# A token-routed expert kernel: tile coefficients picked on ScalarE by expert numbers held in registers, and one empty item left out

## The chip, the cores and the metric

The kernel runs on one core of one Trainium2 chip. The metric is the device time of one execution in microseconds (us). Engines go by the names of the profile: PE is TensorE (matmul) and PEld its weight load, DVE is VectorE, ACT is ScalarE, POOL is GpSimd, SP is SyncE, which here only issues transfers.

## What is computed

For each of 16 x 1024 tokens of width 512: a layernorm; a fixed spectral filter, after which 24 thresholded bits are error-corrected and expanded back to 512 values; and a mixture of 8 experts (512 x 512 each), of which a token uses its best two. The output is `x + s * silu(ffn)`.

```python
logits = x @ router_w.T
probs = jax.nn.softmax(logits, axis=-1)
topk_vals, topk_idx = jax.lax.top_k(probs, K_TOP)          # K_TOP = 2 of 8 experts
topk_w = topk_vals / (topk_vals.sum(-1, keepdims=True) + 1e-06)
...
xn = _layernorm(x, axis=-1)
s = _L0_attn_ref(xn, ...)       # filter, 24 bits, Golay correction, x1 + corrected @ W_le + b_le
g = _silu(_L0_ffn_ref(xn, L0_ffn_router_w, L0_ffn_expert_weights))
x = x + s * g
```

## The kernel before

The work has three stages.

**Routing** (to about 275 us). All tokens are read once; each token's two experts, its weights per expert and its bits are written to a table in HBM (`token_info`), and the tokens are sorted by their unordered pair of experts, of which there are 28. Sorted, they fill 128 tiles of 128 tokens. A main tile is computed with two experts only; where a tile holds tokens of more than one pair, the rest comes from extra items.

**Extra items** (about 275 to 396 us). There are 28 items, one for each pair in `PATH`, each with one expert. An item n gathers 128 token rows (`xbuf`, line 529) and their table rows (`inf`, line 531) on POOL into slot n % 4; DVE folds the rows into sums and differences (`halves_of`, lines 1221 to 1225); ACT rounds them to f16 (`high_part`, line 716) and DVE makes the remainder (`low_part`, line 1231); PE transposes both (`turn_extra`, line 1446), ACT copies the result out of PSUM (`turned_copy`, line 721), PE multiplies by the expert's weights in 12 matmuls (lines 1435 to 1437), ACT scales the product by a per-token coefficient in `cab` (line 737), and DVE adds it to a running sum (line 1251), which SP stores in HBM. The coefficient of an item is one column of the item's table row times one column of `tq`; POOL computes it (`extra_coef`, line 545), one item ahead, just before it gathers. A gather into a slot waits for the coefficient and the remainder of the slot's old item (`coef_ready`, `split_ready`). In the same stage DVE still makes the low halves of the weights (`low_parts`, two instructions of 128x1024, lines 908 and 915), in the order `EXPERT_ORDER`, some of them before the first item and some at the items that `LOW_AT` names.

**Main tiles** (about 396 to 1228 us). A loop over 128 tiles, four to a round. PE reads the tile's two expert numbers from `tile_exp` into registers (`value_load`, line 1460), multiplies by both experts (24 matmuls) and by the filter and bit tables (13 more). DVE combines the two products with the tile's two coefficients `cab[:, k, 0:2]` (lines 1265 and 1274). Those coefficients are made two tiles ahead in two steps: POOL multiplies a mark table `onehot` (128 tiles x 2 experts x 8, with the unscaling of the expert in place of the one) by the 8 weights in the table row (`main_coef`, line 553), and DVE sums over the 8 (line 1239). The mark table itself is built by DVE in the stage of the extra items, in two instructions of 128x2048 elements (`marks_alike`, line 1202, after item 14, and `marks_scaled`, line 1209, after item 18). In each main step POOL adds the input to the result (line 569), multiplies marks (line 553), gathers the rows of four tiles later (lines 529 and 531) and scatters the output (line 535). ACT runs, per step, `high_part`, a copy out of PSUM (line 746), the silu (line 750), the bits (line 707), and the two one-column copies of indices `sidx` (line 755) and `gidx` (line 710), for which POOL's scatter and gather wait.

The engines run their programs in order and meet through semaphores; nothing reorders them. SP transposes the f16 parts of main tiles (`DMA_TRANSPOSE`) and loads the extra sums.

Of the kernel before, what the change touches and what calls it, by code (L numbers as in the profile page):

```python
# [8 lines left out]
F16 = mybir.dt.float16  # L9
# [7 lines left out]
P = 128  # L17
# [61 lines left out]
def build(nc, x_in, W_el, b_el, W_le, b_le, router_w, experts, consts, out):  # L79
# [39 lines left out]
    with ctx:  # L119
# [3 lines left out]
        def sem(name):  # L123
# [61 lines left out]
        tdiag = sb("tdiag", [P, 2, P], F16)  # L185
# [4 lines left out]
        ctmp = sb("ctmp", [P, 2, 2, NE])  # L190
# [58 lines left out]
        onehot = xT4[:, :, :, :].rearrange("p b c n -> p (b c n)")[:, 0:T * 2 * NE].rearrange(  # L249
            "p (t s e) -> p t s e", s=2, e=NE)  # L250
# [11 lines left out]
        z2, t2, g2 = (two(arena, 2 * E * i) for i in range(3))  # L262
        NB = 2 * C + 1
        HB = NB * P // 2
        part_at = (17 * E, 17 * E + HB, 6 * E, 7 * E)
        turn_at = (17 * E + 2 * HB, 17 * E + 3 * HB, 8 * E, 9 * E)
        parts = [arena[:, a:a + (HB if r < 2 else E)].bitcast(F16) for r, a in enumerate(part_at)]
        facing = [arena[:, a:a + (HB if r < 2 else E)].bitcast(F16).rearrange("p (m n) -> p m n", n=P) for r, a in enumerate(turn_at)]
# [19 lines left out]
        def sems(names):  # L288
# [3 lines left out]
        pool_halves, live_ready, marks_ready = sems("pool_halves live_ready marks_ready")  # L292
# [25 lines left out]
        rows_ready, rows_loaded, rows_float, exps_mm, toks_mm, diag_ready, spread_mm, tiles_ready = sems(  # L318
            "rows_ready rows_loaded rows_float exps_mm toks_mm diag_ready spread_mm tiles_ready")
# [7 lines left out]
        coef_mul, coef_sum, coef_ready, x_done, x_scaled, acc_init, acc_ready = sems("coef_mul coef_sum coef_ready x_done x_scaled acc_init acc_ready")  # L327
# [42 lines left out]
        def extra(i):  # L370
            return isinstance(i, int) and i < XR

# [98 lines left out]
        def _(pool):  # L471
# [67 lines left out]
            def extra_coef(n):  # L539

                k = n % U
                pool.wait_ge(ld_x2[k], 32 * (n // U + 1))
                after(pool, x_scaled, n - U + 1)
                c = 8 + PATH[n][1]
                G.tensor_tensor(cab[:, k, 0:1], inf2[:, k, c:c + 1], tq[:, 7, n:n + 1], ALU.mult).then_inc(coef_ready, 1)

            def main_coef(i, k):

                m = (i - XR) * U + k
                pool.wait_ge(ld_x2[k], 32 * (i + 1))  # L550
                if not (first_main(i) and k < 2):
                    pool.wait_ge(coef_sum, m - 1)
                G.tensor_tensor(ctmp[:, k % 2], onehot[:, bass.ds(m, 1)].rearrange("p o s e -> p (o s) e"),
                                inf2[:, k, 8:8 + NE].unsqueeze(1).broadcast_to([P, 2, NE]), ALU.mult).then_inc(coef_mul, 1)

            def extra_prepare(n):
                if n + 1 < NX:
                    extra_coef(n + 1)
                pool.wait_ge(gidx_ready, n + U + 1)
                pool.wait_ge(split_ready, n + 1)  # L560
                pool.wait_ge(coef_ready, n + 1)
                gather(n % U)

            def step(i, k, last=False):
# [5 lines left out]
                if not (last and k + 2 >= U):  # L570
                    main_coef(*at(i, k, 2))
# [8 lines left out]
            for k in range(U):  # L580
                pool.wait_ge(gidx_ready, k + 1)
                gather(k)
            pool.wait_ge(live_ready, 1)
            extra_coef(0)
            for n in range(NX):
                extra_prepare(n)
            pool.wait_ge(marks_ready, 2)
            main_coef(XR, 0)
            main_coef(XR, 1)
# [5 lines left out]
        def _(act):  # L595
# [107 lines left out]
            def bits_part(i, k):  # L703
                b = k % 2
                act.wait_ge(ld_x2[k], 32 * (i + 1))
# [11 lines left out]

            def turned_copy(n):
# [5 lines left out]
            def extra_step(n):  # L724
                k, b = n % U, n % 2
                if 0 < n < NX - 1:
                    turned_copy(n + 1)
# [11 lines left out]
            def step(i, k, last=False):  # L739
# [19 lines left out]
            for k in range(U):  # L759
                gather_index(0, k)  # L760
            act.wait_ge(pad_ready, 1)
            for k in range(3):
                high_part(0, k)
                gather_index(1, k)
                if k == 1:
                    turned_copy(0)
                    turned_copy(1)
            for n in range(NX):
                extra_step(n)
            main_rounds(act, step)  # L770

        @block.vector
        def _(dve):
# [399 lines left out]
            V.memset(again[:, 0:1], 0.0)  # L1173
            V.tensor_scalar(tdiag[:, 0], ident[:, :], tsel[:, 0, 2:3], None, ALU.mult)
            V.tensor_scalar(tdiag[:, 1], ident[:, :], tsel[:, 0, 3:4], None, ALU.mult)
            link(V.tensor_tensor(count, to_tile[:, 0, 0:NX], iota_c[:, 0:NX], ALU.mult))
            V.tensor_reduce(tslot[:, :], count, AXX, ALU.max).then_inc(diag_ready, 1)
# [15 lines left out]
            for c in range(2):  # L1193
                low_parts(c)
            V.memset(acc2[:, 1], 0.0).then_inc(acc_init, 1)

            def marks_alike():
# [3 lines left out]
                dve.wait_ge(spread_mm, 1)  # L1201
# [318 lines left out]
```

## Time and profile before

| | |
|---|---|
| median of 3 runs | 1231.86 us (1228.46 to 1235.25) |
| the profiled execution | 1235.18 us, its span 1233.3 us |
| busy, share of the span | PE 92%, DVE 89%, POOL 71%, ACT 42%, PEld 49% |
| mean granted clock of PE | 0.969 |

Times in the rows below are from the start of the span of the profiled execution. The shares are means over stages that have different limits, so the stages are read one by one.

### The profile page before, as it was taken

To read this page: it belongs to the slowest core of one execution; us is meant where nothing else is said; L and a number is where in the kernel's file an instruction comes from. 1 tells how busy PE (TensorE), PEld (TensorE's weight loads), DVE (VectorE), ACT (ScalarE), POOL (GpSimd) and SP (SyncE) were. 2 spreads that over 40 slices of the span, in tenths; PEclk is the share of its full clock that TensorE was granted. 3 is DMA by queue.
4 is the path that set the end of the run, shared out by engine and by line. 5 is a ranking of instruction groups with operands and counts; after the bars stand their busy time and mean duration, and the time that the engine had idled before them with its cause. 6 is when DMAs were issued, how large, how long until landed. Compare 5 with 4: busy or idle time off the path is not lost. (4 is left out here: it accounts for less than half of the span.)

```text
span 1233.3 us, 26827 instructions
## 1 busy us (share of the span) xinstructions
PE 1131.4 (92%) x6283; PEld 609.0 (49%) x6284; DVE 1096.8 (89%) x2658; ACT 512.7 (42%) x1151; POOL 877.7 (71%) x857
## 2 busy tenths in 40 slices
PE   5998869725889999999999999999999999999996
PEld 4565545412434455555555555555555555555553
DVE  6899969998877889899989998999999899999985
ACT  4476646664655333333333333333333333333332
POOL 1136655648886588777878887888888788888874
PEclk9999989957999999999999999999999999999999
DMA  8669999403446576666667666666666666666663
GB/s 322 242 212 200 198 149 203 81 23 97 150 144 175 147 172 171 171 174 173 174 166 179 173 173 166 176 174 176 172 169 176 171 175 173 170 178 172 174 167 108
DMA packets 216921, 208.74 MB, mean 169 GB/s; under 512 B 166271, under 2 KB 166271, under 8 KB 212786
## 3 DMA queue, kind: packets, MB, share of 16 engines
q1 hardware_dynamic: 184370, 124.31, 42.8%
q0 software_dynamic: 31360, 79.78, 21.9%
q10 hardware_dynamic: 1152, 4.19, 1.3%
q8 instruction: 17, 0.28, 0.1%
q14 instruction: 22, 0.18, 0.1%
HBM read 123.36 MB, written 47.11 MB: 138 GB/s over the span
## 5 line engine op out<-in xcount | busy, mean ns | idle before, releaser
L1435 PE MATMUL banks<-w_hi,arena 128*128 (+1 forms) x1136 | 432.5, 381 | 6.2 <-DMA arena<-arena 5.9
L1436 PE MATMUL banks<-w_lo,arena 128*128 (+1 forms) x1136 | 432.3, 381 | 0.0
L1437 PE MATMUL banks<-w_hi,arena 128*128 (+1 forms) x1136 | 432.2, 380 | 0.0
L716 ACT ACTIVATE arena<-xbuf,inf 128x512 f16<-128x512 f32 x156 | 112.6, 722 | 532.5 <-DVE xbuf L1225 532.2
L529 POOL DMA_INDIRECT xbuf<-in_L_attn_x,gidx x156 | 189.7, 1216 | 78.9 <-issue 66.2
L531 POOL DMA_INDIRECT inf<-token_info,gidx x156 | 200.2, 1283 | 54.0 <-issue 53.4
L508 POOL DMA_INDIRECT pair_tokens<-tok,slot x112 | 112.6, 1005 | 110.4 <-DVE slot L1058 78.4
L569 POOL TENSOR_TENSOR xbuf<-xbuf 128x512 f32<-128x512 f32 x128 | 162.8, 1272 | 35.8 <-DVE xbuf L1294 28.7
L1435 PEld LDWEIGHTS banks<-w_hi,arena 128*128 128x128 f16 x1136 | 111.4, 98 | 134.3 <-issue 17.1
L1437 PEld LDWEIGHTS banks<-w_hi,arena 128*128 128x128 f16 x1136 | 111.5, 98 | 131.5 <-issue 1.7
L535 POOL DMA_INDIRECT out<-xbuf,sidx x128 | 142.6, 1114 | 40.7 <-issue 40.4
L1436 PEld LDWEIGHTS banks<-w_lo,arena 128*128 128x128 f16 x1136 | 111.3, 98 | 117.7 <-issue 1.7
L1221 DVE TENSOR_TENSOR xbuf<-xbuf 128x256 f32<-128x256 f32 x156 | 141.1, 905 | 25.3 <-DMA inf<-token_info,gidx 25.1
L1231 DVE SCALAR_TENSOR_TENSOR arena<-xbuf,inf,arena 128x512 f16<-128x512 f32 x156 | 117.1, 750 | 17.2 <-ACT arena L716 11.5
L1369 PE MATMUL banks<-xT,wcat 128*128 128x512 f32 x256 | 119.8, 612 | 0.8 <-issue 0.4
L1274 DVE SCALAR_TENSOR_TENSOR arena<-banks,cab,arena 128x512 f32<-128x512 f32 x128 | 95.6, 747 | 14.2 <-PE banks L1437 12.2
L1294 DVE TENSOR_TENSOR xbuf<-xbuf,arena 128x512 f32<-128x512 f32 x128 | 88.7, 693 | 17.0
L1265 DVE SCALAR_TENSOR_TENSOR arena<-banks,cab,arena 128x512 f32<-128x512 f32 x128 | 95.9, 749 | 7.3 <-DMA arena<-extra_sums 4.0
L1288 DVE TENSOR_TENSOR xbuf<-xbuf 128x256 f32<-128x256 f32 x256 | 97.5, 422 | 4.4
L928 DVE BATCH_NORM_STATS2 st<-xbuf 128x6 f32<-128x512 f32 x128 | 85.8, 682 | 11.4 <-DMA xbuf<-in_L_attn_x 11.4
L1329 PE MATMUL banks<-ident,xbuf 128*128 128x128 f32 x512 | 73.8, 292 | 22.0 <-DMA xbuf<-in_L_attn_x 21.7
L750 ACT ACTIVATE arena<-arena,inf 128x512 f32<-128x512 f32 x128 | 91.2, 712 | 3.3 <-DVE arena L1274 3.3
(305 smaller groups left out, 1728.7 us busy)
## 6 DMA issues: line engine op xcount, KB each, us to landing
xbuf<-in_L_attn_x SPq DMA_DIRECT2D x32, 1024.0 KB, 11.1
arena<-extra_sums SPq DMA_DIRECT2D x128, 256.0 KB
arena<-in_L_ffn_expert_weights SPq DMA_DIRECT2D x8, 1024.0 KB, 11.0
extra_sums<-arena SPq DMA_DIRECT2D x28, 256.0 KB, 2.9
token_info<-info ACTq DMA_DIRECT2D x8, 512.0 KB, 11.5
xbuf<-in_L_attn_x,gidx POOLq DMA_INDIRECT x156
inf<-token_info,gidx POOLq DMA_INDIRECT x156
arena<-arena SPq DMA_TRANSPOSE x128
```

What stands on the lines that cost most here:

```text
L508: pool.indirect_dma_start(out=pair_slots, out_offset=bass.IndirectOffsetOnAxis(ap=slot[:, buf, t:t + 1], axis=0), in_=tok[:, buf, t:t + 1] ...
L529: pool.indirect_dma_start(out=x2[:, k], out_offset=None, in_=x_rows, in_offset=tokens, bounds_check=N - 1, oob_is_err=False).then_inc(ld_x ...
L531: pool.indirect_dma_start(out=inf2[:, k], out_offset=None, in_=info_dram, in_offset=tokens, bounds_check=N - 1, oob_is_err=False).then_inc ...
L535: pool.indirect_dma_start(out=out_rows, out_offset=bass.IndirectOffsetOnAxis(ap=sidx[:, k:k + 1], axis=0), in_=o2[:, k % 2], in_offset=Non ...
L569: G.tensor_tensor(o2[:, b], sg2[:, b], x2[:, k], ALU.add).then_inc(o_ready, 1)
L716: nc.scalar.activation(hi4[ring(i, k)], uv2[:, b], ACT.Copy, scale=inf2[:, k, 1:2]).then_inc(hi_ready, 1)
L1221: V.tensor_tensor(raw2[:, b, 0:H], x2[:, k, 0:H], x2[:, k, H:E], ALU.add).then_inc(raw_ready, 1)
L1231: V.scalar_tensor_tensor(lo4[ring(i, k)], uv2[:, b], inf2[:, k, 1:2], hi4[ring(i, k)], ALU.mult, ALU.subtract).then_inc(split_ready, 1)
L1369: last = mm(psum[:, 2], wcat[:, c], xT4[:, k % 2, c], start=(c == 0), stop=(c == C - 1))
L1435: mm(ps, hi[:, c], wh, start=(c == 0), stop=False)
L1436: mm(ps, hi[:, c], wl, start=False, stop=False)
L1437: end = mm(ps, lo[:, c], wh, start=False, stop=(c == C - 1))
```

## The change

1. The coefficients of extra items and of main tiles move from POOL to ACT. For an extra item it is one copy of a column with a per-token scale. For a main tile ACT loads each of the two expert numbers into a register and copies column `8 + e` of the table row, scaled by `unscale[:, e]`. There is no sum on DVE for it any more.
2. The mark table is gone: the two DVE instructions that build it, the two that prepare it, one matmul, and 128 multiplications on POOL and 128 sums on DVE.
3. Item 0 (the pair of experts 0 and 1, for which no tokens are ever left over) isn't computed. Its semaphores are counted up, its sum is a memset, and `EXPERT_ORDER` and `LOW_AT` start with expert 2. POOL's first gather is item 1's, and the gather of item 4 goes into the unused slot 0.
4. Some buffers move into the place of the mark table (`xT4`).

```diff
-    EXPERT_ORDER = (*range(1, NE), 0)
-    DIFF_AT = (6, 1, 3, 4, 5, 0, 2, 7)
-    LOW_AT = {1: 4, 2: 5, 3: 6, 9: 7}
+    EXPERT_ORDER = (*range(2, NE), 1, 0)
+    DIFF_AT = (6, 7, 1, 3, 4, 5, 0, 2)
+    LOW_AT = {1: 4, 2: 5, 3: 6, 12: 7}
...
-            def extra_prepare(n):
-                if n + 1 < NX:
-                    extra_coef(n + 1)
+            def extra_gather(n):
+
                 pool.wait_ge(gidx_ready, n + U + 1)
                 pool.wait_ge(split_ready, n + 1)
                 pool.wait_ge(coef_ready, n + 1)
...
                 G.tensor_tensor(o2[:, b], sg2[:, b], x2[:, k], ALU.add).then_inc(o_ready, 1)
-                if not (last and k + 2 >= U):
-                    main_coef(*at(i, k, 2))
                 pool.wait_ge(sidx_ready, m + 1)
...
+            def extra_coef(n):
+
+                k, c = n % U, 8 + PATH[n][1]
+                act.wait_ge(ld_x2[k], landed(n // U, k))
+                after(act, x_scaled, n - U + 1)
+                nc.scalar.activation(cab[:, k, 0:1], inf2[:, k, c:c + 1], ACT.Copy, scale=tq[:, 7, n:n + 1]).then_inc(coef_ready, 1)
+
+            def main_coef(i, k):
+
+                m = (i - XR) * U + k
+                act.wait_ge(ld_x2[k], landed(i, k))
+                if first_main(i):
+                    act.wait_ge(x_scaled, NX - U + k + 1)
+                else:
+                    act.wait_ge(z_ready, m - U + 1)
+                for c in range(2):
+                    e = act.value_load(tile_exp[0:1, c, bass.ds(m, 1)], min_val=0, max_val=NE - 1)
+                    nc.scalar.activation(cab[:, k, c:c + 1], inf2[:, k, bass.ds(e + 8, 1)], ACT.Copy,
+                                         scale=unscale[:, bass.ds(e, 1)]).then_inc(coef_picked, 1)
...
                 elif n + 3 < NX + 2:
                     bits_part(*at(n // U, k, 3))
+                if n + 1 < NX:
+                    extra_coef(n + 1)
                 act.wait_ge(x_done, n + 1)
...
                     bits_part(*at(i, k, 2))
+                    main_coef(*at(i, k, 2))
...
-            def marks_scaled():
-
-                dve.wait_ge(marks_ready, 1)
-                V.tensor_tensor(onehot, onehot, unscale[:, :].unsqueeze(1).unsqueeze(1).broadcast_to([P, T, 2, NE]),
-                                ALU.mult).then_inc(marks_ready, 1)
...
-            for k in range(3):
-                halves_of(0, k)
-                low_part(0, k)
-                if k:
-                    low_parts(k + 1)
-            halves_of(0, 3)
-            for n in range(NX):
+            halves_of(0, 1)
+            halves_of(0, 2)
+            low_part(0, 1)
+            low_part(0, 2)
+            low_parts(1)
+            halves_of(0, 3)
+            low_parts(2)
+            low_part(0, 3)
+            low_parts(3)
+            halves_of(1, 0)
+            for n in range(1, NX):
                 extra_step(n)
```

**POOL in the stage of the extra items.** Before, three rows per item, with the coefficient of the next item first:

```order
50 L545 TENSOR_TENSOR cab<-inf,tq 128x1 [waits ld_x2_2]
51 L529 DMA xbuf<-in_L_attn_x,gidx 128x512 [waits coef_ready,split_ready,gidx_ready]
52 L531 DMA inf<-token_info,gidx 128x64
53 L545 TENSOR_TENSOR cab<-inf,tq 128x1 [waits ld_x2_3]
54 L529 DMA xbuf<-in_L_attn_x,gidx 128x512 [waits coef_ready,split_ready,gidx_ready]
55 L531 DMA inf<-token_info,gidx 128x64
```

Now, where the first three gathers wait only for indices:

```order
42 L531 DMA xbuf<-in_L_attn_x,gidx 128x512 [waits gidx_ready]
43 L533 DMA inf<-token_info,gidx 128x64
44 L531 DMA xbuf<-in_L_attn_x,gidx 128x512 [waits coef_ready,split_ready,gidx_ready]
45 L533 DMA inf<-token_info,gidx 128x64
46 L531 DMA xbuf<-in_L_attn_x,gidx 128x512 [waits coef_ready,split_ready,gidx_ready]
47 L533 DMA inf<-token_info,gidx 128x64
```

The multiplication is gone from POOL, and `coef_ready`, which POOL itself used to fulfil, is now fulfilled by ACT.

**ACT in the same stage.** One item before (its place in the steady part, from the copy of the transposed parts on):

```order
250 L721 ACTIVATE arena<-banks 128x1024 [waits x_done,uvT_done]
251 L716 ACTIVATE arena<-xbuf,inf 128x512 [waits uvT_done,uv_ready]
252 L710 ACTIVATE gidx<-tile_tok 128x1
253 L737 ACTIVATE arena<-banks,cab 128x512 [waits acc_ready,coef_ready,x_done]
254 L721 ACTIVATE arena<-banks 128x1024 [waits x_done,uvT_done]
```

The same now:

```order
252 L718 ACTIVATE arena<-banks 128x1024 [waits x_done,uvT_done]
253 L693 ACTIVATE xT<-xbuf,inf 128x512 [waits uvT_done,uv_ready]
254 L687 ACTIVATE gidx<-tile_tok 128x1
255 L700 ACTIVATE cab<-inf,tq 128x1 [waits x_scaled,ld_x2_1]
256 L736 ACTIVATE xT<-banks,cab 128x512 [waits acc_ready,coef_ready,x_done]
```

The coefficient of item n + 1 now stands behind the rounding (`high_part`) of item n + 3, and ahead of the scaling of item n.

**ACT in the loop over main tiles.** One step before:

```order
404 L716 ACTIVATE arena<-xbuf,inf 128x512 [waits turned1,uv_ready]
405 L743 REGISTER_ALU
406 L746 ACTIVATE xbuf<-banks 128x384 [waits s_ready,y_done]
407 L750 ACTIVATE arena<-arena,inf 128x512 [waits sg_ready,z_ready]
408 L707 ACTIVATE arena<-inf 128x96 [waits turned1,ld_x2_1]
409 L755 ISA [waits stored1]
410 L755 ACTIVATE sidx<-tile_tok 128x1
411 L710 ISA
412 L710 ACTIVATE gidx<-tile_tok 128x1
```

Now, from the bits on:

```order
469 L684 ACTIVATE arena<-inf 128x96 [waits turned1,ld_x2_3]
470 L711 ISA [waits z_ready,ld_x2_3]
471 L711 TENSOR_LOAD tile_exp
472 L711 ISA x2
473 L712 ISA
474 L712 ACTIVATE cab<-inf,unscale 128x1
475 L711 ISA
476 L711 TENSOR_LOAD tile_exp
477 L711 ISA x2
478 L712 ISA
479 L712 ACTIVATE cab<-inf,unscale 128x1
480 L755 ISA [waits stored1]
```

Two loads into a register, some register instructions and two one-column copies stand between the bits and the copies of the indices.

## Rows read from the trace of the kernel before

**Rows 1.** Busy time by stretch: length, then busy and count per engine, clock, DMA

```profile
396.00:1222.00 826.00, 821.21 (x4723) 429.56 (x4723) 751.74 (x1649) 275.11 (x758) 646.76 (x627) 1.00 0.67 171
275.50:393.20 117.70, 93.89 (x562) 45.54 (x561) 98.14 (x210) 67.55 (x115) 101.80 (x93) 0.91 0.46 135
```

**Rows 2.** Groups of ACT, 440 to 1200 us: busy, mean ns, idle before

```profile
L716 ACT ACTIVATE arena<-xbuf,inf 128x512 f16<-128x512 f32 x118 | 85.2, 722 | 457.8 <-DVE xbuf L1225 457.8
```

**Rows 3.** One main step, timeline: start, length, engine

```profile
703.77 0.19 ACT L710 ACTIVATE gidx<-tile_tok 128x1 int32 x1
707.73 0.72 ACT L716 ACTIVATE arena<-xbuf,inf 128x512 f16<-128x512 f32 x1 [3.76 <-DVE xbuf L1225]
...
706.54 0.40 POOL L553 TENSOR_TENSOR ctmp<-xT,inf 128x16 f32<-128x16 f32 x1
707.47 1.15 POOL L529 DMA_INDIRECT xbuf<-in_L_attn_x,gidx  x1 [0.52 <-issue]
```

**Rows 4.** Loads of a register from `tile_exp`, min/median/max ns (lines 1460, 451)

```profile
L1460 PEldq TENSOR_LOAD <-tile_exp x256: 294/344/1192, 390.8 to 1215.4; - x128
L451 SPq FUSED_REGOPS  x248: 46/155/187, 400.9 to 1215.1; - x124
L451 SPq TENSOR_LOAD <-tile_exp x128: 283/728/1049, 400.4 to 1214.6; - x128
```

**Rows 5.** Groups in 315 to 349 us: busy, mean ns, idle before

```profile
L531 POOL DMA_INDIRECT inf<-token_info,gidx x11 | 13.9, 1263 | 3.4 <-issue 3.4
L529 POOL DMA_INDIRECT xbuf<-in_L_attn_x,gidx x10 | 13.7, 1368 | 1.5
...
L545 POOL TENSOR_TENSOR cab<-inf,tq 128x1 f32<-128x1 f32 x10 | 4.0, 395 | 0.3
```

**Rows 6.** Timeline of one extra item, POOL, DVE and ACT

```profile
337.15 1.37 POOL L529 DMA_INDIRECT xbuf<-in_L_attn_x,gidx  x1
338.82 1.02 POOL L531 DMA_INDIRECT inf<-token_info,gidx  x1 [0.30 <-issue]
...
341.65 0.43 DVE L1221 TENSOR_TENSOR xbuf<-xbuf 128x256 f32<-128x256 f32 x1 [0.89 <-DMA inf<-token_info,gidx]
...
342.92 0.72 ACT L716 ACTIVATE arena<-xbuf,inf 128x512 f16<-128x512 f32 x1 [1.06 <-DVE xbuf L1225]
343.55 0.19 ACT L710 ACTIVATE gidx<-tile_tok 128x1 int32<-128x1 int32 x1
343.64 0.67 ACT L737 ACTIVATE arena<-banks,cab 128x512 f32<-128x512 f32 x1
```

**Rows 7.** Timeline of DVE: the first folding instruction of five items

```profile
314.31 0.42 DVE L1221 TENSOR_TENSOR xbuf<-xbuf 128x256 f32<-128x256 f32 x1
...
348.28 0.42 DVE L1221 TENSOR_TENSOR xbuf<-xbuf 128x256 f32<-128x256 f32 x1 [0.97 <-DMA inf<-token_info,gidx]
...
373.05 0.43 DVE L1221 TENSOR_TENSOR xbuf<-xbuf 128x256 f32<-128x256 f32 x1 [0.69 <-DMA inf<-token_info,gidx]
...
389.07 0.42 DVE L1221 TENSOR_TENSOR xbuf<-xbuf 128x256 f32<-128x256 f32 x1 [0.34 <-DMA inf<-token_info,gidx]
```

**Rows 8.** Timeline around the two mark instructions, DVE and POOL

```profile
351.21 2.27 DVE L1202 TENSOR_TENSOR xT<-banks,cst 128x2048 f32<-128x2048 f32 x1
...
353.57 5.73 POOL L529 DMA_INDIRECT xbuf<-in_L_attn_x,gidx  x1
...
367.61 2.29 DVE L1209 TENSOR_TENSOR xT<-xT,unscale 128x2048 f32<-128x2048 f32 x1
...
368.24 3.21 POOL L531 DMA_INDIRECT inf<-token_info,gidx  x1 [0.31 <-issue]
```

**Rows 9.** Timeline of the first items: POOL, then DVE

```profile
276.90 1.95 POOL L531 DMA_INDIRECT inf<-token_info,gidx  x1 [0.30 <-issue]
281.55 1.00 POOL L531 DMA_INDIRECT inf<-token_info,gidx  x1 [0.31 <-issue]
284.25 1.50 POOL L531 DMA_INDIRECT inf<-token_info,gidx  x1 [0.30 <-issue]
...
302.22 1.28 DVE L908 SCALAR_TENSOR_TENSOR w_lo<-w_lo,wscale,w_hi 128x1024 f16<-128x1024 f32 x1
303.42 1.27 DVE L915 SCALAR_TENSOR_TENSOR w_lo<-arena,wscale,w_hi 128x1024 f16<-128x1024 f32 x1
```

**Rows 10.** Timeline, ACT's last scaling and DVE's first work on a main tile

```profile
394.51 0.69 ACT L737 ACTIVATE arena<-banks,cab 128x512 f32<-128x512 f32 x1 [1.90 <-PE banks L1437]
403.98 0.75 DVE L1265 SCALAR_TENSOR_TENSOR arena<-banks,cab,arena 128x512 f32<-128x512 f32 x1 [3.96 <-DMA arena<-extra_sums]
```

More of the change, by code:

```diff
@@ L261, in build @@
         yp2 = raw2[:, :, H:E]
-        z2, t2, g2 = (two(arena, 2 * E * i) for i in range(3))
+        z2, g2 = (two(arena, 2 * E * i) for i in range(2))
+        t2 = two(spare, 4 * E)
         NB = 2 * C + 1
         HB = NB * P // 2
[L265 to L268, printed above, removed]
+        part_at = (17 * E, 17 * E + HB, 0, E)
+        turn_at = (17 * E + 2 * HB, 17 * E + 3 * HB, 2 * E, 3 * E)
+        parts = [(arena[:, a:a + HB] if r < 2 else spare[:, a:a + E]).bitcast(F16) for r, a in enumerate(part_at)]
+        facing = [(arena[:, a:a + HB] if r < 2 else spare[:, a:a + E]).bitcast(F16).rearrange("p (m n) -> p m n", n=P)
+                  for r, a in enumerate(turn_at)]
         hi4, lo4 = [t[:, 0:E] for t in parts], [t[:, E:2 * E] for t in parts]
@@ L371, in extra, with landed @@
             return isinstance(i, int) and i < XR
+        def landed(i, k):
+            return 32 * (i + (1 if k else 0))
         def ring(i, k):
@@ L579, in step @@
                 scatter_out(k)
-            for k in range(U):
+            for k in range(1, U):
                 pool.wait_ge(gidx_ready, k + 1)
                 gather(k)
-            pool.wait_ge(live_ready, 1)
-            extra_coef(0)
             for n in range(NX):
[L586 to L589, printed above, removed]
+                extra_gather(n)
             main_rounds(pool, step)
@@ L758, in _ @@
             act.wait_ge(tiles_ready, 1)
-            for k in range(U):
+            act.sem_inc(gidx_ready, 1)
+            for k in range(1, U):
                 gather_index(0, k)
+            gather_index(1, 0)
+            act.sem_inc(coef_ready, 1)
+            act.sem_inc(hi_ready, 1)
+            act.sem_inc(hl_ready, 1)
+            act.sem_inc(x_scaled, 1)
             act.wait_ge(pad_ready, 1)
-            for k in range(3):
+            act.wait_ge(live_ready, 1)
+            for k in range(1, U):
                 high_part(0, k)
                 gather_index(1, k)
-                if k == 1:
-                    turned_copy(0)
+                if k == 2:
                     turned_copy(1)
-            for n in range(NX):
+                    turned_copy(2)
+            extra_coef(1)
+            for n in range(1, NX):
                 extra_step(n)
+            act.wait_ge(tiles_ready, 2)
+            main_coef(XR, 0)
+            main_coef(XR, 1)
             main_rounds(act, step)
@@ L1277, in step @@
                     low_part(*at(i, k, 2))
-                if not (last and k + 1 >= U):
-                    main_coef(*at(i, k, 1))
                 dve.wait_ge(y_copied, m + 1)
@@ L1486, in step @@
                 end.then_inc(y_done, 1)
-            turn_extra(0)
-            for n in range(NX):
+            pe.sem_inc(uvT_done, 1)
+            pe.sem_inc(x_done, 1)
+            turn_extra(1)
+            for n in range(1, NX):
                 extra_step(n)
```

76 lines of the change are left out of this document (20 added, 56 removed).

## The prediction

> **What bounds the kernel now.** I read the busy time by stretch first, because the page's shares mix three stages. In the main tiles (396 to 1222 us) PE is busy 821.21 of 826 us at full clock, DVE 751.74, POOL 646.76 and ACT 275.11 [rows 1]. The reader is to see that 4.8 us is all that any change off PE can win there, over 128 tiles of 6.45 us. In the extra items (275.5 to 393.2 us) no engine stands at its limit by busy time: PE 93.89 of 117.7, DVE 98.14, POOL 101.80, ACT 67.55. So I went to the groups and the timeline. In the quiet part POOL's only idle time is what the profile calls issue, some 0.3 us before line 531 and nothing to speak of before line 529, while DVE waits for the rows to land, 0.89 us ahead of the item shown [rows 5, 6]. POOL is the bound there, through the time it takes to issue two gathers and one small multiplication. The first folding instruction of an item recurs from 314.31 to 348.28 us ten times over: 3.40 us an item [rows 7]. That is also POOL's sum, 1.37 + 1.26 + 0.40 us of work and some 0.4 us of idle, 3.4 us.
>
> Two places are slower. Up to 314 us DVE is the bound, since it also makes low halves of weights, 2.4 us per expert. Around the mark table the six items from 348.28 to 373.05 us take 24.8 us, 4.13 each [rows 7]: a gather that takes 1.0 us undisturbed lasts 5.73 us right behind the first mark instruction, and another 3.21 us beside the second [rows 8].
>
> **The change, part by part.**
>
> *Main tiles: what leaves.* POOL loses line 553, 0.40 us a step, and DVE its sum of 0.16 us. PE is the bound, so both are worth nothing except where PE waits now, inside the 4.8 us. I take 1 us (bounds 0 and 3).
>
> *Main tiles: what comes.* ACT gets two picks per step. No row shows a pick on ACT. Its parts are a register load, at 0.34 us in the median on PE's sequencer and 0.73 us on SP's, register instructions of 0.05 to 0.16 us, of which there are about three to a pick [rows 4], and a one-column copy, 0.19 us in the index copies [rows 3]. So a pick is between 0.34 + 0.15 + 0.19 = 0.7 us and 1.05 + 0.5 + 0.19 = 1.7 us; I take 1.1, since SP's load feeds the same sort of address arithmetic, and two picks make 2.2 us. Behind them on ACT are the two index copies, for which POOL waits, and then the next step's rounding, for which DVE, SP's transposition and PE wait. The index for the gather is ready at 703.96 us now and would be at 706.2; POOL starts that gather at 707.47 and without line 553 at about 707.0 [rows 3]. The rounding finds ACT idle for 3.76 us in that step, and 457.8 us over 118 steps, 3.88 on average [rows 2, 3]. So two picks are hidden, by 0.8 us on POOL's side and 1.6 on PE's. A gather that comes late by a few tenths feeds a tile four steps later, so the second margin is the one that counts. Cost 0.
>
> *Marks.* DVE loses 2.27 + 2.29 us and two small preparations, and the stretched gathers have nothing to follow. Against the quiet 3.40 us, six items save 24.8 - 20.4 = 4.4 us. The lower bound is 0, if the stretched gathers come from DVE's other work in a row.
>
> Here the Trainium skill is to be weighed. Its page "SBUF — State Buffer", section "SBUF: two separate sides", says that DVE and GpSimd take a shared pair of ports by an exclusive lock for one instruction at a time, and that descriptor writing is kept out by DVE's two-port modes. The row shows 4.7 us of extra time in one gather, twice as long as any one DVE instruction near it, and the first mark instruction had ended before, so a lock held by that one instruction doesn't explain it. If the lock of whatever follows does, the marks matter only by crowding DVE, and the 4.4 us could stay partly in the program: that is the first case of the rival "nothing" below.
>
> *Coefficients of extra items.* POOL loses 28 multiplications of 0.40 us with some 0.15 us around each. If POOL stayed the bound, an item would take 3.40 - 0.5 = 2.9 us. But the gather of item n + 4 waits for the coefficient of item n, which on ACT now stands behind the rounding of item n + 2, and that needs the rows of item n + 2 landed. This is a loop over two items. Its parts: from the end of POOL's line 531 at 339.84 us to DVE's first folding at 341.65, 1.8 us; to ACT's rounding at 342.92, 1.27 us; rounding 0.63 us and index copy 0.09 us until the next instruction starts [rows 6]; the coefficient 0.19 us and a semaphore 0.1 us. That is 4.1 us from the end of one gather to the start of the one two later. The two gathers themselves take 1.37 + 0.30 + 1.02 = 2.7 us there [rows 6], 2.35 undisturbed (1.02 for line 529, as it is in its shortest form). An item takes half the loop: (4.1 + 2.7) / 2 = 3.40 us, between 3.2 and 3.6. So the new wait gives back what the multiplication costs: the releaser of POOL changes, and the pace doesn't. From item 8 to the end of the stage, 21 items, that is 0 (bounds -4 and +4 us); the last five items ran at 16.0 / 5 = 3.2 us before [rows 7], which would be 1 us lost.
>
> *Item 0 and the start.* POOL's first three gathers keep their places; their second halves end at 278.85, 282.55 and 285.75 us [rows 9] and land 1.8 us later, now as items 1 to 3. DVE, in the new order: folding of item 1 from 280.7; of item 2 from 284.4 to 285.6 (it waits for the landing, 2.5 us that item 0's work filled before); two remainders to 287.1; an expert's low halves, 2.4, to 289.5; folding of item 3, 1.2, to 290.7; low halves to 293.1; remainder to 293.8; low halves to 296.2; folding of item 4 to 297.3; folding of item 5, whose gather starts after ACT's coefficient at 291.8 and lands at 296, to 298.5; remainder and sum to 299.8. That point is at 302.22 us now, where line 908 starts [rows 9]. Gain 2.4 us (bounds 1 and 4), less than an item's 3.4, because the start waits for transfers.
>
> *The end of the stage.* ACT's four picks for the first two main tiles start behind its last scaling, which ends at 395.2, and take 4.4 us, and the first sum on DVE that uses them starts at 403.98, held by a transfer [rows 10]. Hidden; without that wait they would cost up to 1 us.
>
> **Sum.** 1 + 0 + 4.4 + 0 - 1 + 2.4 = 6.8 us, taken as 7. The profiled execution took 1235.18 us around a span of 1233.3, so it becomes 1228.2; that execution lies 3.3 us above the median of the runs, 1231.86. Against the median, which I use: **1225 us**. A measurement of this kernel can tell about 0.5%, some 6 us, from no change, so the forecast lies at that edge.
>
> **The rivals.**
>
> *POOL keeps the bound and sheds it.* If landing and rounding overlap better than in the loop above, the pace falls to PE's own 3.05 us (twelve matmuls at 0.216 us and the transpositions at about 0.45), not to 2.9. 21 items x 0.35 us = 7 us more than forecast: about 1218 us. For it: POOL shows no wait but issue. Against: the loop's four durations are all in the rows.
>
> *Nothing is won.* The loop takes 3.6 us an item (+4 us) and the stretched gathers appear elsewhere (+3 us): 1231 to 1232 us. For it: other gathers of 2.7 us stand beside DVE's low halves, which stay. By the page's rule on the lock, taken by itself, the marks' time would partly stay, as said.
>
> *Slower: the picks on ACT.* If a pick takes more than 1.9 us (half of 3.8), ACT's rounding comes late, then DVE's remainder, SP's transposition and PE in every step. At 2.2 us a pick a step grows by 0.6 us: 126 x 0.6 = 76 us, less the 7 won, about 1300 us; at 2.0 us it is 1243. It decides from 1.9 us on, beyond my upper bound of 1.7. For it: no row shows a load on ACT, and one on PE took 1.19 us.
>
> *The change doesn't do what it says*: the order shows that it does, so this has no chance of its own.
>
> **How the numbers follow.** Forecast 0.52, its own range 1221 to 1229; full shedding 0.18; nothing 0.20; slower by the picks 0.10. The range of 8 in 10 goes from 1214 to 1233: it leaves out the slow case and a little below. Faster than 1225.7 holds six tenths of the forecast and the shedding case, 0.49; within 0.5% the rest of the forecast and the case of nothing less a tail, 0.39; slower 0.12.
>
> **What the profile of the changed kernel would show.** Right: the stage of extra items 6 to 7 us shorter, POOL now waiting before line 529 for ACT, an item still near 3.4 us, no gather beyond 3.5 us after 349 us; in the main tiles the same 6.4 us a step, ACT waiting some 1.6 us before its rounding. Wrong: POOL without waits and items near 3.05 us; or ACT not idle before the rounding and PE with gaps in each main step; or gathers of 3 to 6 us still there.

## The result, and the profile after it

The changed kernel is slower. Its median is 1239.88 us (1235.3 to 1243.27) beside 1231.92 us (1227.79 to 1237.16) for the kernel before, a ratio of 1.0066 with a 95% interval of 1.0041 to 1.0091, so 8 us lost where 7 were forecast to be won.

The stage of the extra items is read first, with two rows of the timeline that bound it, POOL's first gather and PE's first matmul of a main tile:

```profile
271.98 1.01 POOL L531 DMA_INDIRECT xbuf<-in_L_attn_x,gidx  x1 [7.95 <-ACT gidx L687]
399.04 0.39 PE L1422 MATMUL banks<-w_hi,arena 128*128 x1 [2.94 <-DMA arena<-arena]
```

The stage takes 127.06 us; before, the same two instructions stood at 275.58 and 395.89, 120.31 us. So 6.75 of the 8 us of loss are here. "The stage" means this length from here on. (The routing ahead of it differs by 3.6 us between the two profiled executions, the other way.) The groups of POOL and DVE in 315 to 385 us:

```profile
L533 POOL DMA_INDIRECT inf<-token_info,gidx x18 | 22.0, 1224 | 5.5 <-issue 5.5
L531 POOL DMA_INDIRECT xbuf<-in_L_attn_x,gidx x18 | 17.9, 997 | 25.1 <-ACT cab L700 22.3 <-issue 2.7
...
L1218 DVE TENSOR_TENSOR xbuf<-xbuf 128x256 f32<-128x256 f32 x18 | 7.6, 422 | 23.7 <-DMA inf<-token_info,gidx 23.7
```

Against [rows 5] POOL has lost the line of multiplications and got 22.3 us of waiting for ACT's coefficient (line 700) in 18 items, and DVE waits as long for the rows to land. No engine is at its limit now; the stretch by engine (length, then busy and count of PE, PEld, DVE, ACT and POOL, clock, DMA):

```profile
318.00:389.00 71.00, 56.59 (x363) 28.61 (x362) 47.20 (x112) 45.98 (x91) 40.34 (x37) 1.00 0.47 144
```

The timeline of two items shows the wait and what it hangs on. POOL's rows, then DVE's and ACT's of the item between:

```profile
349.39 0.99 POOL L531 DMA_INDIRECT xbuf<-in_L_attn_x,gidx  x1 [2.50 <-ACT cab L700]
350.68 1.44 POOL L533 DMA_INDIRECT inf<-token_info,gidx  x1 [0.30 <-issue]
352.43 1.00 POOL L531 DMA_INDIRECT xbuf<-in_L_attn_x,gidx  x1 [0.30 <-issue]
353.73 1.00 POOL L533 DMA_INDIRECT inf<-token_info,gidx  x1 [0.30 <-issue]
357.25 1.00 POOL L531 DMA_INDIRECT xbuf<-in_L_attn_x,gidx  x1 [2.52 <-ACT cab L700]
```

```profile
354.11 0.43 DVE L1218 TENSOR_TENSOR xbuf<-xbuf 128x256 f32<-128x256 f32 x1 [2.40 <-DMA inf<-token_info,gidx]
...
355.37 0.72 ACT L693 ACTIVATE xT<-xbuf,inf 128x512 f16<-128x512 f32 x1 [2.33 <-DVE xbuf L1222]
...
356.00 0.18 ACT L687 ACTIVATE gidx<-tile_tok 128x1 int32<-128x1 int32 x1
...
356.09 0.28 ACT L700 ACTIVATE cab<-inf,tq 128x1 f32<-128x1 f32 x1
```

Every second gather of rows waits: 349.39, 357.25, and on with 7.7 to 8.0 us between them, 7.86 here, which is 3.93 us an item instead of the 3.40 of [rows 7]. The loop closes as the prediction described it: the gather ends at 352.12, lands and is folded from 354.11, rounded from 355.37, its index copied, the old item's coefficient made from 356.09 to 356.37, and the next gather starts at 357.25.

The main tiles are unchanged. PE is busy all the time between 420 and 1215 us, and ACT's two picks stand in the step with room behind them:

```profile
420.00:1215.00 795.00, 793.18 (x4571) 415.61 (x4570) 720.96 (x1482) 327.70 (x983) 595.14 (x494) 1.00 0.68 173
```

```profile
701.89 0.28 ACT L712 ACTIVATE cab<-inf,unscale 128x1 f32 x1
702.44 0.29 ACT L712 ACTIVATE cab<-inf,unscale 128x1 f32 x1 [0.27 <-issue]
702.64 0.19 ACT L755 ACTIVATE sidx<-tile_tok 128x1 int32 x1
702.74 0.19 ACT L687 ACTIVATE gidx<-tile_tok 128x1 int32 x1
705.95 0.72 ACT L693 ACTIVATE arena<-xbuf,inf 128x512 f16<-128x512 f32 x1 [3.03 <-DVE xbuf L1222]
```

Two picks put off the index by 0.85 us (701.89 to 702.74) and leave 3.03 us of waiting before the rounding, where [rows 3] had 3.76.

### The profile page after: what moved, and what is told of

Its sections match the earlier page's. It is cut to its first block and busy times, and to the rows that moved or that the text cites. A ratio compares the mean times of both kernels' runs of the same rounds, so it can differ in the third digit from the quotient of the medians.

```text
span 1238.1 us, 27677 instructions
## 1 busy us (share of the span) xinstructions
PE 1128.5 (91%) x6262; PEld 606.6 (49%) x6263; DVE 1077.8 (87%) x2519; ACT 577.9 (47%) x1431; POOL 808.5 (65%) x699
## 5 line engine op out<-in xcount | busy, mean ns | idle before, releaser
L1422 PE MATMUL banks<-w_hi,arena 128*128 (+1 forms) x1076 | 410.1, 381 | 8.1 <-DMA arena<-arena 7.1
L1423 PE MATMUL banks<-w_lo,arena 128*128 (+1 forms) x1076 | 409.5, 381 | 0.0
L1424 PE MATMUL banks<-w_hi,arena 128*128 (+1 forms) x1076 | 409.4, 381 | 0.0
L693 ACT ACTIVATE arena<-xbuf,inf 128x512 f16<-128x512 f32 x141 | 101.8, 722 | 407.7 <-DVE xbuf L1222 407.6
L531 POOL DMA_INDIRECT xbuf<-in_L_attn_x,gidx x155 | 173.9, 1122 | 161.1 <-POOL xbuf L553 96.8
L1422 PEld LDWEIGHTS banks<-w_hi,arena 128*128 128x128 f16 x1076 | 105.6, 98 | 130.9 <-issue 18.6
L1424 PEld LDWEIGHTS banks<-w_hi,arena 128*128 128x128 f16 x1076 | 105.7, 98 | 124.4 <-issue 1.9
L1423 PEld LDWEIGHTS banks<-w_lo,arena 128*128 128x128 f16 x1076 | 105.5, 98 | 112.2 <-issue 1.8
L1261 DVE SCALAR_TENSOR_TENSOR arena<-banks,cab,xT 128x512 f32<-128x512 f32 x128 | 95.9, 749 | 21.7 <-PE banks L1424 17.3
L1228 DVE SCALAR_TENSOR_TENSOR arena<-xbuf,inf,arena 128x512 f16<-128x512 f32 x141 | 105.6, 749 | 7.3 <-ACT arena L693 4.3
L1252 DVE SCALAR_TENSOR_TENSOR xT<-banks,cab,arena 128x512 f32<-128x512 f32 x128 | 95.8, 749 | 8.6 <-DMA arena<-extra_sums 6.0
L712 ACT ACTIVATE cab<-inf,unscale 128x1 f32 x256 | 73.9, 289 | 43.7 <-issue 43.3
```

What stands on the lines that cost most here:

```text
L531: pool.indirect_dma_start(out=x2[:, k], out_offset=None, in_=x_rows, in_offset=tokens, bounds_check=N - 1, oob_is_err=False).then_inc(ld_x ...
L693: nc.scalar.activation(hi4[ring(i, k)], uv2[:, b], ACT.Copy, scale=inf2[:, k, 1:2]).then_inc(hi_ready, 1)
L1228: V.scalar_tensor_tensor(lo4[ring(i, k)], uv2[:, b], inf2[:, k, 1:2], hi4[ring(i, k)], ALU.mult, ALU.subtract).then_inc(split_ready, 1)
L1422: mm(ps, hi[:, c], wh, start=(c == 0), stop=False)
L1423: mm(ps, hi[:, c], wl, start=False, stop=False)
L1424: end = mm(ps, lo[:, c], wh, start=False, stop=(c == C - 1))
```

## The experiments

Twelve kernels were run in three groups of four; the kernel before ran beside each group, and the ratio is to it. Its median was 1300.81 us in the first group, on a chip where the routing takes about 60 us longer, 1223.89 in the second and 1224.14 in the third, so times are compared within a group and ratios across them.

### The coefficient first in ACT's step (e1)

```diff
                 k, b = n % U, n % 2
+                if n + 1 < NX:
+                    extra_coef(n + 1)
                 if 1 < n < NX - 1:
                     turned_copy(n + 1)
                 if n + 3 < NX + 2:
                     high_part(*at(n // U, k, 3))
...
-                if n + 1 < NX:
-                    extra_coef(n + 1)
                 act.wait_ge(x_done, n + 1)
```

> The changed kernel with one move on ScalarE: in each step of the extra items the coefficient of item n + 1 is made first, before the copy of the transposed parts and before the rounding of item n + 3. Theory, the loop: in the changed kernel a gather waits for a coefficient that stands behind a rounding two items on, and the loop of two items takes 7.86 us. With the coefficient first the loop spans three items, so GpSimd should no longer wait some 2.5 us for it in every second item, an item should take 3.1 to 3.3 us and the stage from the first gather to PE's first main matmul should fall from 127.1 us to about 112: about 1225 us, ratio to before 0.99 to 1.00. Rival, the picks in the main tiles cost the time: nothing changes, 1240 us. Rival, something else holds the extra items (VectorE, the start without item 0): an item stays above 3.7 us.

Measured: 0.992 (0.9898 to 0.9942), stage 109.73 us. Groups of POOL in its steady stretch, 383 to 442 us:

```profile
L531 POOL DMA_INDIRECT xbuf<-in_L_attn_x,gidx x18 | 22.9, 1270 | 9.2 <-issue 6.8 <-ACT cab L700 2.1 <-DVE arena L1228 0.3
L533 POOL DMA_INDIRECT inf<-token_info,gidx x18 | 20.3, 1128 | 5.5 <-issue 5.2 <-ACT cab L700 0.3
```

The wait for ACT falls from 22.3 to 2.4 us over 18 items. The coefficient itself takes the same time (0.28 us in both kernels); only its place has changed.

### The coefficient three items ahead (e2), and back on POOL (e3)

In e2 the same call stands where the changed kernel has it, but makes the coefficient of item `n + 3`, whose own rounding it follows:

```diff
-                if n + 1 < NX:
-                    extra_coef(n + 1)
+                if n + 3 < NX:
+                    extra_coef(n + 3)
...
                 gather_index(1, k)
+                extra_coef(k)
...
-            extra_coef(1)
             for n in range(1, NX):
```

The last lines are the start of the stage, where each of the items 1 to 3 gets its coefficient behind its own rounding.

> The changed kernel, but the coefficient of item n + 3 is made right behind the rounding of the same item, two steps earlier than in the changed kernel, and at the start each of items 1 to 3 has its coefficient right behind its rounding. Loop theory: the wait is gone as in the run with the coefficient first, and at the start the gather of item 5 no longer waits 3.4 us; as fast as that run or 1 to 3 us faster, about 1223 us. Rival, picks in the main tiles: 1240 us. If this is as slow as the changed kernel and the run with the coefficient first is too, the loop theory falls.

In e3 the coefficient is POOL's again, as before, while item 0, the marks and the main picks stay changed:

```diff
             def extra_gather(n):
+                if n + 1 < NX:
+                    pool_coef(n + 1)
                 pool.wait_ge(gidx_ready, n + U + 1)
...
-                if n + 1 < NX:
-                    extra_coef(n + 1)
                 act.wait_ge(x_done, n + 1)
```

> The changed kernel with the coefficients of the extra items back on GpSimd as before the change; the picks of the main tiles stay on ScalarE, there is no mark table and no item 0. Loop theory: the multiplication of 0.4 us comes back and the wait goes, an item takes 3.4 us in the quiet part as before; with marks gone (4.4 us) and the shorter start (2 to 4 us) the stage takes about 113 us, the time is about 1225 us. Rival, the picks on ScalarE in the main tiles: 1238 us or more, with main tiles slower than 6.45 us each.

Measured: e2 0.9929 (0.9912 to 0.9947), stage 108.66 us; e3 0.9947 (0.9928 to 0.9967), stage 111.57 us. Both are rid of the loss. e3 against before also gives the terms for the marks, item 0 and the main tiles together: 5.3 parts in a thousand, 6.5 us of 1231 (4 to 9); the forecast had 4.4 + 2.4 + 1 = 7.8.

### The kernel before with the added wait alone (e4)

```diff
                 pool.wait_ge(coef_ready, n + 1)
+                pool.wait_ge(hi_ready, n + 3)
                 gather(n % U)
```

> The kernel before the change with one more wait and nothing else: GpSimd's gather of item n + 4 waits until ScalarE has rounded item n + 2. Coefficients, marks and item 0 stay as they were. Loop theory: landing 2.0 + to the rounding 1.26 + rounding 0.7 + from ScalarE's end to the start of a gather that waited 0.9 + two gathers 2.74 make 7.6 us, an item takes about 3.8 us in place of 3.40, so the kernel becomes 6 to 10 us slower than before, ratio about 1.006. Rival, the wait is harmless and the loss came with another part of the change: ratio 1.000.

Measured: 1.0066 (1.0045 to 1.0087), stage 125.65 us. Two gathers that waited, and the rounding that released the second:

```profile
378.27 1.03 POOL L529 DMA_INDIRECT xbuf<-in_L_attn_x,gidx  x1 [0.94 <-ACT gidx L711]
...
381.46 1.03 POOL L529 DMA_INDIRECT xbuf<-in_L_attn_x,gidx  x1 [0.27 <-issue]
...
383.57 0.72 ACT L717 ACTIVATE arena<-xbuf,inf 128x512 f16<-128x512 f32 x1 [1.35 <-DVE xbuf L1226]
...
385.17 1.03 POOL L529 DMA_INDIRECT xbuf<-in_L_attn_x,gidx  x1 [0.93 <-ACT gidx L711]
```

One line that computes nothing makes the kernel before as slow as the changed one. The profile puts the wait down to the index copy, which is the last thing ACT finished; what the added line waits for is the rounding, and that ends at 384.29, 0.88 us before the gather starts.

The pace isn't the one that I expected. Two items take 6.90 us here (378.27 to 385.17) and 7.03 us the next time, 3.5 us an item and not 3.8. The gather of a table row takes 1.09 us and is folded 1.62 us after its end, where my sum had 1.44 and 2.0; no run shows why they are shorter here. Of the 5.3 us by which the stage is longer, 2.2 arise at the start (the low halves of item 1 end 31.3 us after the first gather instead of 29.1), and the rest comes after the last low halves, where the kernel before had been faster than 3.40 (the last six intervals between gathers are 3.49 us on average instead of 3.13). So e4 shows that such a wait is enough for a loss of this size. It doesn't confirm the 3.93 us of the changed kernel, which rests on that kernel's own rows.

### The wait moved to the gather that needs it (e5), and the changed kernel beside it (e8)

The coefficient reads the table row, so only the gather of table rows must wait for it:

```diff
                 pool.wait_ge(split_ready, n + 1)
...
+                pool.indirect_dma_start(out=x2[:, k], out_offset=None, in_=x_rows, in_offset=tokens,
+                                        bounds_check=N - 1, oob_is_err=False).then_inc(ld_x2[k], 16)
                 pool.wait_ge(coef_ready, n + 1)
-                gather(n % U)
+                pool.indirect_dma_start(out=inf2[:, k], out_offset=None, in_=info_dram, in_offset=tokens,
+                                        bounds_check=N - 1, oob_is_err=False).then_inc(ld_x2[k], 16)
```

> The changed kernel with one wait moved: the gather of the rows no longer waits for the coefficient, only the gather of the table row does, since only that one overwrites what the coefficient reads. Theory of the loop over two items: only the table gather is then in it, 5.13 us from landing to the released gather plus 1.0 to 1.4 for the gather itself, 6.1 to 6.6 us for two items, so 3.05 to 3.3 us an item in place of 3.93, the stage 13 to 17 us shorter than that of the changed kernel (127.1), time about 0.993 to 0.996 of before. Rival: a gather that waits for another engine costs its 0.9 us whatever the loop, because POOL starts again each time; then an item still takes 3.7 us or more and the ratio is 1.002 or above.

> The changed kernel itself, unaltered, on the chip of these runs, so that the ratios of the others can be set against it. Its earlier ratio was 1.0066 of before; both theories expect 1.004 to 1.009 here, an item of 3.93 us in the steady part and a stage of about 127 us.

Measured: e5 0.99 (0.9883 to 0.9917), 1211.93 us, stage 108.94 us; e8 1.0062 (1.0045 to 1.0078), 1230.75 us, stage 127.69 us. Moving one wait by one instruction is worth 18.8 us, in the time and in the stage, a little more than the 13 to 17 that I had expected. In e5 one wait of this kind in POOL's timeline:

```profile
340.44 1.00 POOL L547 DMA_INDIRECT xbuf<-in_L_attn_x,gidx  x1 [0.30 <-issue]
342.77 1.19 POOL L550 DMA_INDIRECT inf<-token_info,gidx  x1 [1.33 <-ACT cab L705]
```

and the stretch by engine, where PE is busy for 53.35 of 55 us and is now what bounds it:

```profile
310.00:365.00 55.00, 53.35 (x344) 26.93 (x343) 44.99 (x104) 43.55 (x87) 41.13 (x35) 1.00 0.58 174
```

A released gather still costs its 0.8 us (ACT's copy ends at 342.00), so the rival, that the cost comes with each wait whatever the loop, is false: it was paid only where it stood in the loop.

### Both edits (e9), and the marks' work put back (e6 on e1, e10 on e9)

```diff
+                if n in (NX // 2, NX // 2 + 4):
+                    V.tensor_tensor(spare[:, 6 * E:8 * E].bitcast(F16).rearrange("p (t s e) -> p t s e", s=2, e=NE),
+                                    unscale[:, :].unsqueeze(1).unsqueeze(1).broadcast_to([P, T, 2, NE]),
+                                    iota_c[:, 0:NE].unsqueeze(1).unsqueeze(1).broadcast_to([P, T, 2, NE]), ALU.mult)
```

The result of these two instructions is unused.

> The version with the coefficient first in ACT's step (ratio 0.992, stage 109.7 us), with two unused DVE instructions of 128x2048 put back after items 14 and 18, where the mark table was built. My marks term of 4.4 us says: a gather of 3 to 6 us appears behind each, and the stage grows by 4 to 5 us (113.7 to 114.7), ratio about 0.9955. Rival: the stretched gathers come from DVE's work in a row whatever it is, and POOL now has slack; then the stage grows by 0 to 2 us and the ratio stays within 0.001 of 0.992.

> The changed kernel with the two edits that each took away the loop put together: the coefficient first in ACT's step, and the wait for it only before the gather of the table row. If PE's pace of 3.05 us an item is the floor in both, together they win nothing more: ratio 0.990 to 0.993, stage 108 to 110 us, no gather waiting for ACT beyond the first items. Rival: some of the wait is left in either alone; then 2 to 4 us more come off, ratio 0.987 to 0.989.

> The version with both edits, with the two unused DVE instructions of 128x2048 put back at the places where the mark table was built; run beside that version, so that the marks' price is a difference on one chip. My term of 4.4 us: stage 4 to 5 us longer than that of the version without them, ratio 0.0035 higher. Rival, that POOL's slack takes up the stretched gathers once it doesn't bound the stage: stage 0 to 2 us longer, ratio within 0.0015.

Measured: e6 0.9951 (0.9934 to 0.9968), stage 112.24 us, beside 0.992 for e1 in another group; e9 0.9915 (0.9888 to 0.9941), 1213.95 us, stage 113.31 us; e10 0.995 (0.9931 to 0.9969), 1216.65 us, stage 115.12 us. DVE's two instructions and POOL's gathers in e10:

```profile
333.06 2.27 DVE L1306 TENSOR_TENSOR xT<-unscale,cst 128x2048 f16<-128x2048 f32 x1
333.85 4.81 POOL L550 DMA_INDIRECT inf<-token_info,gidx  x1 [0.30 <-issue]
...
348.08 4.35 POOL L550 DMA_INDIRECT inf<-token_info,gidx  x1 [0.30 <-DVE arena L1233]
348.60 2.29 DVE L1306 TENSOR_TENSOR xT<-unscale,cst 128x2048 f16<-128x2048 f32 x1
```

The long gathers of [rows 8] are back, in both kernels, so this work does bring them. But they are not its alone. In e9, without any such instruction, the profiled execution has this one beside an expert's low half:

```profile
327.14 3.35 POOL L547 DMA_INDIRECT xbuf<-in_L_attn_x,gidx  x1 [0.30 <-DVE xT L1233]
327.67 1.29 DVE L931 SCALAR_TENSOR_TENSOR w_lo<-arena,wscale,w_hi 128x1024 f16<-128x1024 f32 x1
```

and its stage is 113.31 us, while e11 and e12 below, the same program up to the main tiles, have 108.02 and 107.94. So the stage scatters by 5 us between single profiles. The marks' price is 2.7 us by the medians of e9 and e10 and 4.3 by their ratios, whose intervals overlap a little. A price of 4.4 is not refuted, and not measured closely either. By its ratio e9 also wins nothing over e1 and e5, as expected if either edit alone brings the stage to PE's pace.

### More picks in the main tiles: four (e11), six (e12), ten (e7)

```diff
+                for j in range(2):          # 4 in e12, 8 in e7
+                    e = act.value_load(tile_exp[0:1, j % 2, bass.ds(m, 1)], ...)
+                    nc.scalar.activation(unused[:, k, j:j + 1], inf2[:, k, bass.ds(e + 8, 1)], ACT.Copy,
+                                         scale=unscale[:, bass.ds(e, 1)])
                 for c in range(2):
```

e11 and e12 are built on e9, e7 on e1. These picks are unused.

> The version with the coefficient first in ACT's step, with eight unused picks ahead of the two real ones in every main step (their columns go to an unused buffer). Two picks take 0.85 us in the changed kernel, so ten take 4.3 us, 3.4 us more than the real two, and ACT waits 2.8 to 3.0 us before its rounding. Theory that ACT's slack is what that wait shows: a step grows by about 0.5 us, 126 steps by 60 us, ratio 1.04. Rival one: the work ahead gives more room than that wait shows, ratio below 1.005. Rival two: POOL's gather, which waits for the index copy behind the picks, is the sooner limit, a step grows by 1 us or more, ratio above 1.08.

> The version with both edits, with two unused picks ahead of the real ones in every main step. In the version with ten picks one took 0.68 us with its idle time, so two more take 1.4 us out of some 3.0 us for which ACT waits before its rounding. Theory that this wait is ACT's slack: no change, ratio within 0.001 of the version without them, and a wait of 1.5 to 1.7 us left. Rival, that a pick delays what is behind it beyond ACT's own time (POOL's gather by the index copy): a step grows by 0.2 us or more, ratio 0.02 higher.

> The same with four unused picks, 2.7 us out of the 3.0 us. Theory: still no change beyond 0.003, a wait of 0.2 to 0.5 us left before the rounding; the limit lies between here and the ten picks. If ACT's slack is used up earlier, because the instructions of the picks hold up the ones behind them, a step grows by 0.3 us or more, ratio 0.03 higher.

Measured: e11 0.9902 (0.9873 to 0.9932), no change; e12 1.0473 (1.0448 to 1.0499); e7 1.351 (1.3479 to 1.3541). The groups of ACT in the main tiles, of e11 over 107 steps and of e12 over 99:

```profile
L699 ACT ACTIVATE arena<-xbuf,inf 128x512 f16<-128x512 f32 x107 | 77.3, 722 | 173.4 <-DVE xbuf L1232 173.4
...
L722 ACT ACTIVATE cab<-inf,unscale 128x1 f32 x216 | 63.6, 294 | 87.4 <-issue 87.4
L718 ACT ACTIVATE unused<-inf,unscale 128x1 f32 x215 | 62.0, 288 | 36.7 <-issue 36.7
```

```profile
L718 ACT ACTIVATE unused<-inf,unscale 128x1 f32 x396 | 114.1, 292 | 100.1 <-issue 99.8
L699 ACT ACTIVATE arena<-xbuf,inf 128x512 f16<-128x512 f32 x99 | 71.3, 720 | 89.7 <-DVE xbuf L1232 84.4 <-issue 5.2
...
L722 ACT ACTIVATE cab<-inf,unscale 128x1 f32 x197 | 58.0, 295 | 131.8 <-issue 131.8
```

Busy and idle time added, a step's picks cost 0.90 us for two (e9), 2.33 for four and 4.08 for six. With four, ACT waits 1.62 us before the rounding instead of 3.04, and nothing else changes. With six a step takes 0.56 us more ((1281.9 - 1210.77) / 126), which my expectation for e12 denied: 0.9 us of ACT's wait is still left, but POOL's gather now waits for the index copy behind the picks, and PE for what comes later still. Groups of POOL, DVE and PE in e12:

```profile
L532 POOL DMA_INDIRECT xbuf<-in_L_attn_x,gidx x99 | 116.7, 1179 | 155.5 <-ACT gidx L693 107.0 <-POOL xbuf L559 39.1 <-issue 9.4
...
L1228 DVE TENSOR_TENSOR xbuf<-xbuf 128x256 f32<-128x256 f32 x99 | 85.9, 868 | 83.7 <-DMA inf<-token_info,gidx 83.7
...
L1432 PE MATMUL banks<-w_hi,arena 128*128 x792 | 303.0, 383 | 40.7 <-DMA arena<-arena 39.1 <-issue 0.5
```

So POOL's side is the nearer margin, as the rows read; no run here moved the index copies ahead of the picks to prove it.

In e7 ACT itself is the bound. Its groups over 74 steps:

```profile
L713 ACT ACTIVATE unused<-inf,unscale 128x1 f32 x592 | 168.1, 292 | 236.6 <-issue 236.4
L694 ACT ACTIVATE arena<-xbuf,inf 128x512 f16<-128x512 f32 x74 | 53.1, 718 | 52.0 <-issue 50.7 <-DVE xbuf L1227 1.3
...
L717 ACT ACTIVATE cab<-inf,unscale 128x1 f32 x146 | 43.0, 295 | 59.0 <-issue 59.0
```

Of 52.0 us of idle time before its rounding 50.7 are issue, so ACT hardly waits for anyone. A pick there costs 0.69 us, not the 0.43 from which I had expected 60 us. Ten picks take 6.9 us a step, 6.0 more than two, and the idle time before the rounding falls from 3.04 to 0.70 us. That makes 3.7 us more, about the 3.5 us by which a step is longer than in e5 ((1652.69 - 1211.93) / 126). The ratio is the one that my second rival had asked for (above 1.08), but its reason, POOL's gather as the sooner limit, is not what these rows show.

## Why the prediction was wrong, point by point

**The step that failed** is the loop in *Coefficients of extra items*. "The coefficient 0.19 us and a semaphore 0.1 us. That is 4.1 us from the end of one gather to the start of the one two later" and from it "the releaser of POOL changes, and the pace doesn't". The form of the loop was right, instruction for instruction. Its size was not: from 352.12 to 357.25 it is 5.13 us. Landing took 1.99 us for 1.8, folding 1.26 for 1.27, rounding and index copy the 0.72 foretold, the coefficient 0.28 for 0.19, and from its end to the start of the gather 0.88 us for 0.1. With the two gathers and the 0.30 us between them, 2.73 us, that is 7.86 us for two items, 3.93 us each. The 0.88 us is the largest part of what was missing, 0.8 of 1.0 us, and half of it an item. It stood in the trace of before, in two rows that I didn't quote, where a gather waits for ACT's index copy:

```profile
274.48 0.48 ACT L710 ACTIVATE gidx<-tile_tok 128x1 int32<-128x1 int32 x4 [3.30 <-DVE tile_tok L1169]
275.58 1.02 POOL L529 DMA_INDIRECT xbuf<-in_L_attn_x,gidx  x1 [8.74 <-ACT gidx L710]
```

The four copies run from 274.48 to 274.96. The first gather needs only the first of them, which ends at 274.68, and it starts 0.90 us after that, 0.62 us after the end of the last. I had taken 0.1 us from no row at all. With 0.6 to 0.9 the loop would have come out at 3.65 to 3.8 us an item, 5 to 8 us over 21 items, and the forecast at no change.

0.53 us on the 23 items from item 5 on is 12.2 us. This is an estimate: from the gather of item 13 to that of item 27 an item takes 3.93 us, but before that DVE's low halves set part of the pace in both kernels. Between the end of the low halves at item 1 and the first main matmul the forecast had 3.4 us won; it was 10.6 lost. So the loop is some 12 us of a miss of 14.0 us; the rest I didn't take apart. That the loop and nothing else turned the sign is shown by e1, e2 and e5, each of which breaks it in another way, leaves the rest of the change as it is, and lands at 0.990 to 0.993. e4 adds that such a wait alone can cost as much.

**"POOL keeps the bound and sheds it"**, 1218 us, described what happens once the loop is away: PE's own pace. e5 stands 12 us below before, where that rival had 14.

**"Nothing is won"** named the right mechanism, a loop of more than 3.40 us an item, and gave it 3.6; the place was right and the size short again.

**Marks**, 4.4 us: their stretched gathers are away in the changed kernel (none over 1.53 us after 349 us), and come back with the work. By e3 this, the start and the main tiles are worth 6.5 us together. **Item 0 and the start**, 2.4 us: the end of item 1's low halves is 25.3 us after the first gather and was 29.1, 3.8 us won, inside its bounds. **Main tiles, what leaves**, 1 us: not seen; from first to last main matmul 829.2 us beside 827.7, where single profiles scatter by as much. **What comes**, 0: right. I had put two picks at 2.2 us where they take 0.9, and e11 shows that 2.3 us would have been hidden too. **"Slower: the picks on ACT"** put its threshold at 3.8 us for a step's picks; e12 has 4.08 and is slower, so the limit was near where it was said to be, but the changed kernel is nowhere near it. As the rows of e12 read, it was reached on POOL's side, by the late index, which the prediction had said would not count. The example in that rival is also added up wrongly: at 2.0 us a pick it should be 0.2 x 126 = 25 us, less the 7, so 1250 us and not 1243.

## What to carry to other kernels

When work moves to another engine, a slot's release moves with it: draw the loop from the release through the transfer and back, and price each handover in it by a row in which that very kind of instruction waits for another engine. Then ask which of the waiting instructions really overwrites what is read; here the first of two gathers waited for a reader of the second, and one line was worth 18.8 us. In a program in order, put a short instruction on which another engine waits ahead of the long one that waits itself.

## What the hardware showed that I had not expected

- A gather on POOL that has waited for ACT in the extra items starts 0.88 us after the end of the instruction that releases it in the changed kernel (all 13 times) and in e4, 0.76 to 0.77 us in e5, where it is the gather of table rows. A gather of table rows that waits for nothing starts 0.30 us after the gather before it. Behind POOL's own addition in the main tiles it is 0.87 us too:

```profile
703.46 1.27 POOL L553 TENSOR_TENSOR xbuf<-xbuf 128x512 f32<-128x512 f32 x1
705.60 1.13 POOL L531 DMA_INDIRECT xbuf<-in_L_attn_x,gidx  x1 [0.87 <-POOL xbuf L553]
```

- What a pick by register costs depends on its place and on how many there are: 0.45 us each for two in a step, 0.72 for each of the next two, 0.87 for the two after, 0.69 on average where there are ten. The one-column copy itself is busy for 0.29 us each time; the rest is issue.
- In e10 a gather of 4.81 us starts 0.79 us after the start of a 2.27 us instruction of the kind `tensor_tensor` and goes on 3.3 us beyond its end. While this gather runs, DVE runs only instructions of the kinds `tensor_tensor` and `scalar_tensor_tensor`. The Trainium skill, page "SBUF — State Buffer", section "Who interferes with whom", says that `tensor_tensor` has no two-port mode, and infers that descriptor generation isn't held up by it. This row and [rows 8] speak against that inference as a rule, and no run here shows what holds the gather instead.
- With PE waiting in each step (e7) its granted clock is 0.89 on average, a mixture of stretches at 2.4 and at 1.2 GHz, where the changed kernel's main tiles have 1.00. The experts' matmuls take 418 to 425 ns there instead of 379. Since ACT is the bound in e7, no run shows whether that lengthens the step.

```profile
750.00:1050.00 300.00, 223.47 (x1117) 107.80 (x1118) 160.60 (x363) 146.35 (x483) 140.99 (x120) 0.89 0.44 113
```
